# State space heads: squares of a group's four heads summed on VectorE, one product with ones per step

## The reference, cut to what matters

```python
y = (Y_diag + Y_off).reshape(b, s, H, P) + D_res
y = y.reshape(b, s, I)
gs = I // G                                   # 512: four heads
h32 = y * jax.nn.silu(gate.astype(jnp.float32))
g = h32.reshape(b, s, I // gs, gs)
var = jnp.mean(g * g, axis=-1, keepdims=True)
h32 = (g * jax.lax.rsqrt(var + EPS)).reshape(b, s, I)
return norm_w * h32 @ out_proj_w.T
```

## Time and profile before

| | us |
|---|---|
| median of 3 runs | 3485.99 |
| lowest, highest | 3485.69, 3489.45 |
| the profiled execution | 3490.39 |
| its span | 3488.6 |
| TensorE busy in it | 2766.1 |
| VectorE busy | 1854.6 |
| ScalarE busy | 1553.7 |
| GpSimd busy | 1204.1 |

### The profile page before, as it was taken

How to read it: one execution, slowest core, us unless ns; L and a number is a source line. 1 busy time by engine, 2 the same in 40 slices (tenths; PEclk the granted TensorE clock), 3 DMA queues, 4 the chain that set the end, 5 groups by cost and what they waited for, 6 DMA issues and landing times. The chain is left out here.

```text
span 3488.6 us, 49109 instructions
## 1 busy us (share of the span) xinstructions
PE 2766.1 (79%) x13661; PEld 1696.1 (49%) x13663; DVE 1854.6 (53%) x4142; ACT 1553.7 (45%) x3112; POOL 1204.1 (35%) x1132
## 2 busy tenths in 40 slices
PE   5799999879999975887887937887477525988884
PEld 2477777646777753444444513333344212455552
DVE  4676666666666656767773156774322510222334
ACT  3555555455555543767771115665155200123331
POOL 1477777437777740000000021000100063144443
PEclk8999999989999985555557957998679755899997
DMA  1122111012122106500000000000000051377875
GB/s 61 46 55 51 34 51 37 7 49 55 27 53 55 37 12 208 170 1 0 1 1 29 0 17 1 1 1 1 21 1 0 1 179 69 69 163 169 180 172 124
DMA packets 127079, 192.70 MB, mean 55 GB/s; under 512 B 17552, under 2 KB 88208, under 8 KB 125584
## 3 DMA queue, kind: packets, MB, share of 16 engines
q1 hardware_dynamic: 83696, 134.71, 13.7%
q0 software_dynamic: 23616, 33.24, 5.4%
q10 hardware_dynamic: 19584, 22.57, 2.4%
HBM read 123.23 MB, written 67.25 MB: 55 GB/s over the span
## 5 line engine op out<-in xcount | busy, mean ns | idle before, releaser
L228 DVE SCALAR_TENSOR_TENSOR h_pre<-h_px,h_par,h_pre 128x510 f32<-128x510 f32 (+2 forms) x384 | 286.5, 746 | 270.6 <-ACT h_pre L689 250.7
L843 POOL TENSOR_TENSOR norm_rstd<-norm_mv,mhalf 128x4 f32<-128x4 f32 x24 | 28.2, 1177 | 1023.3 <-DVE norm_mv L826 1023.3
L652 PE MATMUL h_po<-h_wo,h_h 128*128 128x256 f32 x1024 | 329.3, 412 | 0.0
L2906 POOL DMA_INDIRECT moe_sums<-ex_y,ex_sidx x132 | 204.8, 1552 | 321.1 <-DVE ex_y L3074 302.9
L574 POOL TENSOR_SCALAR h_decay<-h_cumb,h_sel 128x256 f32<-128x256 f32 x256 | 292.0, 1141 | 25.4 <-DMA h_cumb<-cum_rows 25.4
L585 POOL TENSOR_TENSOR h_mix<-h_decay,cb 128x768 f32<-128x768 f32 x128 | 232.9, 1820 | 166.3 <-ACT h_decay L675 166.3
L616 PE MATMUL h_px<-x_cols,h_w 128*128 128x512 f32 x512 | 254.4, 620 | 25.6 <-DMA h_d<-d_skip 25.6
L1256 ACT ACTIVATE xq_ex<-xq_ps,xq_nmax,xq_qs 128x512 f32<-128x512 f32 x256 | 199.4, 779 | 113.6 <-DVE xq_nmax L1324 113.0
L621 PE MATMUL h_pz<-x_cols,h_w 128*128 128x512 f32 x512 | 242.4, 596 | 5.7 <-DVE h_gate L742 5.6
L1322 DVE TENSOR_REDUCE xq_top<-xq_ps 128x1 f32<-128x512 f32 x256 | 176.3, 689 | 83.5 <-PE xq_ps L1169 81.7
L701 ACT ACTIVATE h_xt<-h_pxt,h_sel 128x128 f32<-128x128 f32 x512 | 146.4, 369 | 152.2 <-PE h_pxt L640 152.2
(11 more groups left out here) (390 smaller groups left out, 6004.6 us busy)
## 6 DMA issues: line engine op xcount, KB each, us to landing
h_cumb<-cum_rows SPq DMA_DIRECT2D x32, 1024.0 KB, 8.6
moe_tiles<-blank SPq DMA_DIRECT2D x4, 6642.0 KB, 44.1
ex_w<-moe_w SPq DMA_DIRECT2D x64, 352.0 KB
ex_xg<-moe_tiles ACTq DMA_DIRECT2D x136, 162.0 KB
ex_wd<-moe_wd SPq DMA_DIRECT2D x64, 176.0 KB
h_w<-w_xg SPq DMA_DIRECT2D x8, 1024.0 KB, 10.4
moe_sums<-blank SPq DMA_DIRECT2D x2, 2176.0 KB, 26.7
h_wo<-w_out SPq DMA_DIRECT2D x8, 512.0 KB, 10.3
```

The source lines that it names most:

```text
L228: ins = dve.scalar_tensor_tensor(out=out[:, :, back:S], in0=src[:, :, 0:S - back], scalar=par[:, at + CK - 1 - back:at + CK - back], in1=o ...
L652: pe.matmul(po[t // TPB][:, t % TPB, :], hh[j % 2][:, t * P:(t + 1) * P], w_out[s.pg][:, j, :], start=(j == 0 and t % TPB == 0), stop=(j = ...
L2906: pool.indirect_dma_start(out=r.sums[i % 2][:, :], out_offset=bass.IndirectOffsetOnAxis(ap=sidx[i][:, 0:1], axis=0), in_=y[i % 2][:], in_o ...
```

## The change

`out` issues the four products with the output weights alone. ScalarE's square of head 0 goes into a new tile sqsum (two buffers, by step), those of heads 1 to 3 into h_sq as before. VectorE adds h_sq to sqsum for heads 1 to 3 (`gather`), between silu and the taps of the same slot, behind a wait for the square and a drain. After the last head's output products TensorE waits for the third addition and issues four products of sqsum with ones. ScalarE's wait for h_sq to be free is now one for the addition, and for sqsum one for TensorE's `out` two steps back.

```diff
--- before.py
+++ after.py
@@ -481,6 +481,7 @@
         y = sb("y", [P, 2 * S])
         hh = [sb(f"h{i}", [P, 2 * S]) for i in range(2)]
         sq = [sb(f"sq{i}", [P, 2 * S]) for i in range(2)]
+        sqsum = [sb(f"sqsum{i}", [P, 2 * S]) for i in range(2)]
         var = sb("var", [P, TW])
         rstd = sb("rstd", [P, TW])
         px = [psum(f"px{i}", [P, 2, S]) for i in range(2)]
@@ -509,6 +510,7 @@
         scanned = sem("scanned")
         finished = sem("finished")
         squared = sem("squared")
+        summed = sem("summed")
         outed = sem("outed")
         vared = sem("vared")
         rooted = sem("rooted")
@@ -642,17 +644,20 @@
 
             def out(s, j, h):
                 pe.wait_ge(finished, LEAD + h + 1)
-                pe.wait_ge(squared, LEAD + h + 1)
                 if j == 0:
 
                     pe.wait_ge(added, LEAD + s.n)
                     pe.wait_ge(scaled, LEAD + s.g + 1)
                 for t in range(TW):
 
-                    pe.matmul(po[t // TPB][:, t % TPB, :], hh[j % 2][:, t * P:(t + 1) * P], w_out[s.pg][:, j, :],
-                              start=(j == 0 and t % TPB == 0), stop=(j == HG - 1), skip_group_check=True)
-                    mm = pe.matmul(pss[:, t:t + 1], sq[j % 2][:, t * P:(t + 1) * P], r.ones[:, 0:1],
-                                   start=(j == 0 and t == 0), stop=(j == HG - 1), skip_group_check=True)
+                    mm = pe.matmul(po[t // TPB][:, t % TPB, :], hh[j % 2][:, t * P:(t + 1) * P], w_out[s.pg][:, j, :],
+                                   start=(j == 0 and t % TPB == 0), stop=(j == HG - 1), skip_group_check=True)
+                if j == HG - 1:
+
+                    pe.wait_ge(summed, LEAD + (s.n + 1) * (HG - 1))
+                    for t in range(TW):
+                        mm = pe.matmul(pss[:, t:t + 1], sqsum[s.vb][:, t * P:(t + 1) * P], r.ones[:, 0:1],
+                                       start=(t == 0), stop=(t == TW - 1), skip_group_check=True)
                 mm.then_inc(outed, 1)
 
             parts = ((3, project), (1, scan), (2, turn), (0, out))
@@ -677,8 +682,11 @@
             def square(s, j, h):
                 act.wait_ge(finished, LEAD + h + 1)
 
-                act.wait_ge(outed, LEAD + h - 1)
-                act.activation(sq[j % 2][:], hh[j % 2][:], ACT.Square).then_inc(squared, 1)
+                if j == 0:
+                    act.wait_ge(outed, LEAD + (s.n - 1) * HG)
+                else:
+                    act.wait_ge(summed, LEAD + s.n * (HG - 1) + j - 2)
+                act.activation(sqsum[s.vb][:] if j == 0 else sq[j % 2][:], hh[j % 2][:], ACT.Square).then_inc(squared, 1)
 
             def activate(s, j, h):
                 if s.opens and j == 0:
@@ -720,7 +728,7 @@
             for one in po:
                 dve.memset(one[:], 0.0)
             dve.memset(pss[:, 0:TW], 0.0)
-            for one in (picked, convolved, opened, silued, finished):
+            for one in (picked, convolved, opened, silued, finished, summed):
                 dve.drain().then_inc(one, LEAD)
             dve.drain().then_inc(vared, LEAD - 1)
             dve.drain().then_inc(added, LEAD - 1)
@@ -758,6 +766,12 @@
 
                 dve.wait_ge(outed, LEAD + h - 1)
                 dve.tensor_tensor(hh[j % 2][:], y[:], gate[j][:], ALU.mult).then_inc(finished, 1)
+
+            def gather(s, j, h):
+                if j:
+                    dve.wait_ge(squared, LEAD + h + 1)
+                    dve.drain()
+                    dve.tensor_tensor(sqsum[s.vb][:], sqsum[s.vb][:], sq[j % 2][:], ALU.add).then_inc(summed, 1)
 
             def variance(s):
                 dve.wait_ge(outed, LEAD + (s.n + 1) * HG)
@@ -782,7 +796,7 @@
                         if nxt:
                             select(nxt)
                         add(prev)
-                    slot(((3, conv), (3, open_)), cur, nxt, j)
+                    slot(((0, gather), (3, conv), (3, open_)), cur, nxt, j)
 
             first = Step(0, 0, 0, 0)
             select(first)
```

## The result

| us | before | changed |
|---|---|---|
| median of 4 runs each | 3487.72 | 3443.16 |
| lowest, highest | 3485.69, 3490.55 | 3439.73, 3446.63 |
| the profiled execution | 3490.39 | 3441.67 |
| its span | 3488.6 | 3439.5 |
| first h_h to last h_h, first and second stage | 481.8, 483.2 | 460.6, 458.4 |

The changed kernel takes 0.9872 of the time, interval 0.9855 to 0.9889: 44.6 us less by the medians, where 83 were forecast, and 6 us above the range. The last line of the table is read from the first and last start of h_h in each stage. The two stages give 46 us (964.9 to 919.0 together); what lies outside of them moved by 3. So the whole gain lies where it was expected, and a little more than half of it is there.

What follows compares the result with a forecast made beforehand. TensorE was taken to bound both stages of heads; -86.4 us for removed products, +2.7 for heads at each half's start and +0.6 for group changes gave -83, so a median of 3403 us, range 3394 to 3437.

Steps and rivals of the forecast that it cites:

- What bounds the kernel: In both stages of heads TensorE is busy almost throughout and sets the pace; work taken from its queue shortens the time.
- Part 1: TensorE's ones products for three of four heads go: 384 products at 0.225 us each, 86.4 us saved.
- The rival at 0.14: On TensorE, each removed narrow product saves only 0.14 us: 54 us in all, 3432 us; chance 7%.
- Part 2: The four remaining ones products, in a row at the fourth head's end on TensorE, still cost 0.225 us each.
- Part 3: 96 additions on VectorE, 0.69 us each before the taps, 66 us of new work, fit idle time and cost nothing.
- a ring of 6.4 us: Taps, tanh, h_decay, h_mix and addition, should the addition sit out h_mix: 6.4 us, under the 6.9 slot, no cost.
- GpSimd's step, 27.1: GpSimd's own loop over four heads, with h_mix, h_decay products, ScalarE's h_decay and h_rstd: 27.1 us, under 28.5.
- The tolerance of 2.8 us: VectorE may run 2.8 us late with h_gate before TensorE stops at the next slot's pz.
- Part 4: TensorE's new wait for summed has 4.6 us of cover; each of six group changes is allowed 0.1 us.
- The sum: Whole kernel: -86.4, +2.7 for heads at each half's start, +0.6 for group changes, giving -83 us.
- The 11% rival: VectorE becomes the bound in the heads: slowed additions sit out h_mix, step 30.0, gain 38 us, 3448 us; chance 11%.
- Both signs: Signs of a wrong forecast: TensorE idle before pz or scan with VectorE as releaser; additions longer than 0.9 us.

## Why the prediction was wrong

*What bounds the kernel.* Right. TensorE sets the slots, and without the additions, or with one operand of them in PSUM, the stages lose 79 to 80 us.

*Part 1, what the removed products cost.* Right: 0.225 us each. Slots of 6.9 were seen in three experiments (no addition, operand in PSUM, addition behind the gate), po products 0.43 apart. The rival at 0.14 has fallen.

*Part 2, the four in a row.* Right: 0.81 us and some 0.09 at the next px, 0.90 taken.

*Part 3, the addition.* This is the step that failed. I took 0.69 us, perhaps 0.87, from one meeting, an h_h beside an h_decay product. The product that the addition would meet was another, h_mix, with two SBUF operands; the rows showed no meeting of that kind, and I let the nearest one stand for it. I then allowed for the addition to sit out h_mix and found a ring of 6.4 us, "no cost". That ring was mis-sized. On the same path the changed kernel takes 7.15, from the taps at 549.14 to the next at 556.29: taps 2.41, then 1.20 in place of my 0.52 to the start of h_decay, h_decay 0.99, h_mix 2.08 in place of 1.81, and 0.47 from its end to the taps. The 1.20 holds the tanh and a wait of 0.56 for GpSimd's last product. So the step that failed is that a meeting was charged to VectorE alone. Nothing was put on GpSimd's side, where the products behind the addition lose 0.43 us a head, and nothing on the other op with two SBUF operands, h_xs, in which h_mix now starts and loses 0.26. My own figure for GpSimd's step, 27.1, becomes 27.1 + 3 x 0.43 = 28.4 with the first, and 29.2 with both, over TensorE's 28.5; 29.0 was measured. (The tolerance of 2.8 us comes out at 3.0 from its own two numbers, 8.7 and 5.7; nothing hangs on it.)

I had also set aside the rule of the Trainium skill, "SBUF — State Buffer", section "SBUF: two separate sides", that the op which starts first keeps the other out for its whole length, as not borne out by these rows. The traces agree with it in two of three cases. A VectorE op with two SBUF operands that starts inside h_mix ends 0.55 us behind h_mix, all 92 times in the changed kernel. A GpSimd op that starts inside such a VectorE op is held almost to its end: with 0.40 us of h_xs to go h_mix loses 0.26, with 0.57 of an addition to go the h_decay product loses 0.43. What the traces don't bear out is that a VectorE op which starts inside an h_decay product waits for all of it: an addition there took 0.69 to 0.81, the h_h of the earlier trace rows 0.87, an h_xs at most 0.97 beside a product of 1.14. That meeting is the one that I had read.

*Part 4, the waits.* TensorE's new wait for the sum cost nothing, as said. The change of group did: I allowed 0.1 us for each of six, and it is 2.7. That followed from part 3, since only a GpSimd with room to spare can take 2.1 us of extra work, and without the additions the steps behind catch up all but 0.5.

*The sum.* In the profiled pair the stages lack 33 us of the 79: some 16 from 32 steps of 29.0 in place of 28.5, some 13 from six changes of group (2.7 in place of 0.5 each), the rest at the starts and ends of the stages. Of the 83, 4 was not there to begin with.

*The rivals.* The 11% rival, VectorE as the bound, came out at 3448 and so nearest. Its mechanism, an addition held up by h_mix, is part of what was seen; but it priced the first head at 8.4 (7.57 measured), left GpSimd out, and knew nothing of the groups, so its number is near by errors that cancel. Both signs that I had named for it were seen: additions longer than 0.9, and TensorE held at pz by h_gate, 42 times and 15.1 us in the weight loads' rows.

## What to carry to other kernels

Work that is moved to an engine with room has to be laid beside what the other engines do at that moment. Here a VectorE op with two SBUF operands and a GpSimd op could not run together where the GpSimd op was h_mix, or where the VectorE op was first: the later one waited, and both queues paid, in different ops. Look at the op behind as well as at the op beside. Put such an op where the other engine is idle or runs a one-operand op, or give it an operand in PSUM; and judge it in the slot that you want to reach, since in the old one it may be free. If a product with one column is dear, look at its weight loads and its type first: a narrower type there took away as much as the whole regrouping was to.

## What the hardware did that was not expected

Less work made the loop slower, twice: 0.5 us less a head on GpSimd gave steps of 29.9, a tap less on VectorE 29.6, against 29.0. The hold depends on who starts first. An h_xs or an addition that starts inside h_mix takes 1.5 to 2.3 us and, in the changed kernel and in the one before with the additions, ends 0.55 behind it, wherever inside it started; where h_xs is already running, it is h_mix that pays, up to 2.23 in place of 1.81 in the changed kernel. And the same addition with one operand in PSUM takes 0.69 in the very same place.
